# The last of eight gates moved out of the attention loop, into the loop's drain, the feed-forward layer's tail and the convolutions

## The chip, the cores and the metric

The kernel runs on one NeuronCore of one Trainium2 chip. Its engines work side by side and wait for each other on semaphores: TensorE (PE, with its weight loads as PEld), VectorE (DVE), ScalarE (ACT), GpSimd (POOL) and SyncE (SP, which issues DMAs). The metric is the device time of one execution in microseconds (us), the median of several runs.

## The reference

Two transformer layers over x of 4 x 256 tokens by 256 channels. The input of every sublayer goes through a gate, so there are four gates. Cut to what matters:

```
# a gate: r is x, k and v are the side input f, time_emb the condition
tf    = sigmoid(sum(time_emb));  decay = exp(-exp(w)) * (0.5 + 0.5*tf)
ek    = exp(min(k, 30));         ekv = ek * v
nf, df = forward  scans over tokens:  a = a*decay + ekv_t ;  b = b*decay + ek_t
nb, db = the same scans backward
euk   = exp(min(u + k, 30))
num   = nf + nb - ekv + euk*v ;  den = df + db - ek + euk
gate  = sigmoid(r) * num / max(den, 1e-8) * (0.8 + 0.2*tf)

layer 0:  x += attention(gate0(x))           16 heads of 16, causal softmax
          x += ternary_ffn(gate1(x))          256 -> 1024 -> 256, quantised
layer 1:  x += ssd(gate2(x))                  in-projection, convolution of width 4, chunked
                                              state space with 64 heads, gated norm, out-projection
          x += moe(gate3(x))                  8 experts, top 2
```

Only sigmoid(r) depends on x. The rest of a gate (scans, numerator, denominator, quotient) depends on inputs alone and can be computed at any time before it is used.

## The kernel before

Channels lie on the 128 partitions (2 tiles of 128), the 1024 tokens on the free axis in two halves of 512. A **gate** in what follows is one of eight pieces of work, i = 2m + c, for gate m = 0..3 of the reference and token half c = 0, 1. Its result, the quotient, goes to R[:, m, c]. Gate 7 (m = 3, c = 1) is therefore used last of all, in `gate_tiles` ahead of the experts.

On VectorE a gate is cut in steps (`gate_step(i, k)`), each on 128 x 1024 elements in float32. Step 1 is the forward and the backward scan of the denominator (L959 and L962, with a small product at L961 between them), step 2 the same two scans of the numerator, step 0 the denominator's sum (L966), step 3 two instructions for the numerator (L968, L969), step 5 two of a Newton step on the reciprocal (L973, L974), and step 6 the product into R (L976). ScalarE supplies what they read: `decay` (the decay matrix), `scaled_inputs`, `bonus` (the exponential with u), and `reciprocal_guess` (three activations over 128 x 1024, L549 to L551).

The order of instructions on each engine is written out by hand; there is no scheduler. The attention is a loop over 32 **units** u: unit u is 4 of the 16 heads (u mod 4) for one tile of 128 queries (u // 4). Tiles with odd number look at 256 keys and those with even number at 128. In iteration u

- PE does scores(u+1) (L1534, L1538), the transposition of unit u-1 (L1553), the values of unit u-2 (L1571, L1578), and after every fourth unit a projection of 16 matmuls (L1469);
- DVE does `inverse_sums` in odd u (L1037), `maxima(u)` (L1050), every fourth unit `add_attention` (L1033, which adds a projection to x and so waits for it), then the gate parts, and in even u `normalise` (L1042);
- ACT does the exponentials of unit u (`weigh`, L614), the copy of the transposed unit u-1 (L601), the turned sums (L605), and its own gate parts.

scores(u+1) waits until unit u-1's exponentials are done, because it overwrites their bank. Which gate parts go with which unit is set by PARTS: part n belongs to gate i = 1 + n // 5 with k = n % 5, and DVE does for k = 0, 1, 2, 3 the steps 0, 2, 3 and 5 with 6, and for k = 4 step 1 of the next gate. There are 35 parts for 32 units, so three units (TWICE = 6, 15, 24) have two.

After unit 31 comes the **drain** (the last transposition, values, projection and additions), then the feed-forward layer over 8 token tiles in a software pipeline of 14 stages s, then the state space sublayer: dt (L1196 to L1200), six convolutions (L1208; XBC_ORDER), during which ACT applies silu to each convolved tile (L753) and to the gate bank of one token tile (`gate_silu`, L742), whose bank PE (`gate_in`, L1755) can then refill; then the chunk loop (`front`, from L1234), and last the experts, whose weights are fetched while they compute. The scratch area `arena` (30 K words a partition) is shared by hand between the stages: in the kernel before, the feed-forward layer's buffers lie over the gates' inputs fT, fc, ek, ekv and their sums, so a gate can't be under way while that layer runs.

## Time and profile before

| | us |
|---|---|
| median of 3 runs | 668.86 (668.79 to 670.04) |
| time of the profiled execution | 668.92 |
| its span (first to last instruction) | 667.1 |
| PE busy | 530.3 (79%) |
| DVE busy | 410.8 (62%) |
| ACT busy | 371.0 (56%) |
| POOL busy | 147.9 (22%) |

1.8 us lie between the profiled execution's span and its time. In the span the attention takes from about 42 to 224 us, the feed-forward layer until about 304, the in-projection and convolutions until 345, the chunk loop until 465, and the rest is routing and experts. Times in the rows below are counted from the start of the span. Busy shares of the whole span mix these stages, so they say little of one; what a stage is worth is read in its own stretch.

### The profile page before, as it was taken

How to read it: one execution, taken by the hardware profiler on the slowest of the kernel's cores; microseconds unless marked ns; L12 is line 12 of the kernel's file. 1: busy time of each engine (PE TensorE's matmuls, PEld its weight loads, DVE VectorE, ACT ScalarE, POOL GpSimd, SP SyncE). 2: the span in 40 equal slices, each digit the busy share in tenths (PEclk: the TensorE clock that was granted, in tenths of full speed). 3: DMA queues.
4: the chain of work that ended last, by engine and by line, in shares of the span. 5: the costliest groups of instructions: out<-in, count | busy, mean ns of one | idle time of the engine just before them, and what ended most of it. 6: DMA issues, size and time to landing. Idle time of an engine off the chain costs nothing.

```text
span 667.1 us, 14042 instructions
## 1 busy us (share of the span) xinstructions
PE 530.3 (79%) x5730; PEld 384.8 (58%) x5732; DVE 410.8 (62%) x620; ACT 371.0 (56%) x793; POOL 147.9 (22%) x115
## 2 busy tenths in 40 slices
PE   0386988887687766579989999998469999999980
PEld 0153655665465652364664566557469999996560
DVE  7989999999988477975955646546811111111223
ACT  7996888978876407656667565585312222222212
POOL 1000000000000127830229666220022222222110
PEclk9985599787867898989999999999679999999995
DMA  8600000000000000000000000000579999888815
GB/s 330 215 2 0 1 1 1 2 1 1 1 1 33 1 0 1 0 1 1 2 2 3 2 3 2 3 2 2 190 274 420 420 420 352 321 311 322 345 78 197
DMA packets 18335, 71.18 MB, mean 107 GB/s; under 512 B 4832, under 2 KB 9696, under 8 KB 14688
## 3 DMA queue, kind: packets, MB, share of 16 engines
q1 hardware_dynamic: 15120, 64.00, 25.1%
q0 software_dynamic: 1920, 5.25, 2.1%
q10 hardware_dynamic: 1232, 1.06, 0.5%
q8 instruction: 45, 0.74, 0.5%
q14 instruction: 18, 0.15, 0.1%
HBM read 65.57 MB, written 4.72 MB: 105 GB/s over the span
## 4 chain that ended last, share of the span: by engine, by line
PE 52%; DVE 35%; ACT 6%; issue 4%; DMA 2%; POOL 1%; SPq 0%; DVEq 0%; POOLq 0%; ACTq 0%
PE PS L1469 37%; DVE arena L962 5%; DVE arena L959 4%; DVE nmx L1050 3%; PE PS L1982 2%; PE PS L1799 2%; PE PS L2051 2%; PE PS L1755 1%; PE PS L1617 1%; DVE R L976 1%; DVE arena L974 1%; DVE arena L973 1%; DVE arena L968 1%; DVE arena L969 1%; ACT arena L781 1%
## 5 line engine op out<-in xcount | busy, mean ns | idle before, releaser
L1469 PE MATMUL PS<-arena 128*128 128x128 f32 (+5 forms) x1374 | 160.1, 293 | 17.7 <-DVE arena L1147 10.1
L1469 PEld LDWEIGHTS PS<-arena 128*128 128x128 f32 (+4 forms) x1376 | 126.7, 164 | 44.6 <-issue 25.9
L614 ACT ACTIVATE arena<-PS,nmx 128x128 f32<-128x128 f32 (+1 forms) x128 | 52.1, 423 | 30.2 <-DVE nmx L1050 30.2
L1417 DVE TENSOR_TENSOR R<-arena,PS 128x128 f32<-128x128 f32 x16 | 4.6, 288 | 88.2 <-ACT arena L878 88.2
L389 POOL TENSOR_SCALAR arena<-ident,gcol 128x128 f32<-128x128 f32 x4 | 2.4, 602 | 213.5 <-DMA gcol<-in_gcol 213.5
L481 POOL DMA_INDIRECT ypair<-arena,oid x20 | 19.8, 988 | 121.9 <-ACT arena L884 121.9
L1534 PE MATMUL PS<-arena 32*128 32x128 f32 (+1 forms) x128 | 23.7, 454 | 27.0 <-ACT arena L614 27.0
L449 POOL TENSOR_TENSOR arena<-arena 128x1024 f32<-128x1024 f32 x16 | 37.8, 2371 | 32.8 <-DVE arena L1235 26.8
L1469 PE MATMUL PS<-arena,R 128*128 128x256 f32 x192 | 44.2, 380 | 0.6 <-ACT arena L884 0.6
L1469 PEld LDWEIGHTS PS<-arena,R 128*128 128x128 f32 x192 | 35.2, 190 | 5.1 <-issue 1.0
L962 DVE TENSOR_TENSOR_SCAN arena<-dmat,arena 128x1023 f32<-128x1023 f32 x16 | 37.6, 2348 | 0.6
L1553 PE MATMUL PS<-ident,arena 128*128 128x128 f32 x192 | 35.5, 336 | 0.5 <-ACT arena L601 0.5
L884 ACT ACTIVATE arena<-PS 128x256 f32<-128x256 f32 x20 | 7.7, 384 | 49.4 <-PE PS L1469 36.1
L1534 PEld LDWEIGHTS PS<-arena 32*128 32x128 f32 x128 | 11.6, 220 | 35.9 <-ACT arena L614 33.2
L1050 DVE TENSOR_REDUCE nmx<-PS 128x4 f32<-128x512 f32 (+1 forms) x32 | 30.6, 958 | 1.6 <-PE PS L1538 0.5
L1553 PEld LDWEIGHTS PS<-ident,arena 128*128 128x128 f32 x192 | 29.6, 177 | 3.2 <-issue 2.2
L471 POOL DMA_INDIRECT arena<-arow,gid x20 | 19.6, 981 | 49.5 <-DVE gid L1390 43.7
L871 ACT ACTIVATE arena<-PS 128x512 f32<-128x512 f32 (+1 forms) x20 | 11.9, 597 | 32.7 <-PE PS L1469 26.8
L860 ACT ACTIVATE arena<-PS 128x256 f32<-128x256 f32 x20 | 7.7, 384 | 37.8 <-PE PS L1963 37.8
L614 ACT ACTIVATION_READ_ACCUMULATOR arena<-PS,nmx 128x1 f32 x128 | 26.6, 208 | 0.0
L670 ACT ACTIVATE arena<-PS,oscale 128x512 f32<-128x512 f32 x16 | 10.6, 682 | 24.6 <-PE PS L1469 24.1
L1208 DVE SCALAR_TENSOR_TENSOR arena<-PS,convw,arena 128x1020 f32<-128x1020 f32 (+2 forms) x18 | 23.0, 1276 | 0.7
(312 smaller groups left out, 1181.0 us busy)
## 6 DMA issues: line engine op xcount, KB each, us to landing
arena<-in_moe SPq DMA_DIRECT2D x23, 1408.0 KB, 7.2
arena<-in_moe SPq DMA_DIRECT2D x23, 768.0 KB, 9.6
inproj<-in_inproj SPq DMA_DIRECT2D x1, 1344.0 KB, 10.5
arena<-in_fT SPq DMA_DIRECT2D x2, 512.0 KB, 4.2
R<-in_w1T SPq DMA_DIRECT2D x1, 1024.0 KB, 7.7
R<-in_w2T SPq DMA_DIRECT2D x1, 1024.0 KB, 9.7
R<-in_w3T SPq DMA_DIRECT2D x1, 1024.0 KB, 11.7
xT<-in_xT SPq DMA_DIRECT2D x1, 1024.0 KB, 13.7
```

The costliest lines, as they stand in the source:

```text
L449: pool.tensor_tensor(part, part, gm[i % 2].unsqueeze(1).broadcast_to([P, 32, Q]), ALU.mult).then_inc(S["pool_m"], 1)
L471: pool.indirect_dma_start(xin[:, s % XR, :], None, arow, bass.IndirectOffsetOnAxis(ap=gid[:, b:b + 1], axis=0)).then_inc(ld_xin[s % XR], 16)
L481: pool.indirect_dma_start(ypair, bass.IndirectOffsetOnAxis(ap=oid[:, b:b + 1], axis=0), yb[s % YB], None).then_inc(st_y, 16)
L614: sc.activation(pr[u % 2][:, j, 0:n], PS[:, 2 * (u % 2) + j // 2, (j % 2) * 256:(j % 2) * 256 + n], ACT.Exp, bias=nmx[:, u % 2, j:j + 1], ...
L959: done(v.tensor_tensor_scan(y, dmat[:, 0:N], x, 0.0, ALU.mult, ALU.add))
L962: done(v.tensor_tensor_scan(y[:, 0:N - 1][:, ::-1], dmat[:, 1:N][:, ::-1], y[:, 0:N - 1][:, ::-1], y[:, N - 1:N], ALU.mult, ALU.add), "dve ...
L1050: done(v.tensor_reduce(nmx[:, u % 2, :], src[:, :, 0:P * (tt + 1)], X, ALU.max, negate=True), "dve_max")
L1208: done(v.scalar_tensor_tensor(o[:, :, back:], s[:, :, 0:T - back], convw[:, k, 3 - back:4 - back], o[:, :, back:], ALU.mult, ALU.add), "dv ...
L1469: last = mm(dst, l, r, start=(n == 0), stop=(n == len(pairs) - 1))
L1534: mm(PS[:, 2 * (u % 2) + j // 2, (j % 2) * 256:(j % 2) * 256 + n], qT[j % 2][r:r + 32, ch, ct, t:t + P], kT[r:r + 32, ch, ct, (b % 2) * T: ...
L1553: last = nc.tensor.transpose(PSB[:, 4 * HALF + c:4 * HALF + c + P], pr[u % 2][:, j, k * P:(k + 1) * P], ident[:])
L1799: last = mm(PS[cols[c], r, :], ugt[rows, rows], stp[i % 2][rows, 32 * c + 16 * j:32 * c + 16 * j + 16, :].rearrange("p h t -> p (h t)"), s ...
```

## The change

Gate 7 leaves the loop. PARTS now holds 30 parts, one for each of the units 0 to 29; units 30 and 31 have none, and unit 29's part has only ScalarE's work. Step 1 of gate 7 is split: the forward scan goes between unit 31's maxima and the last `inverse_sums`, the backward scan after `add_attention(6)`; step 0 follows the last `normalise`. Step 2 is split as well: the forward scan at stage 12 of the feed-forward layer, ahead of the last addition (L1139), the backward one behind `gate(2, 1)`. Step 3 lies between the two halves of the dt computation, and steps 5 and 6 behind the last convolution. On ACT `reciprocal_guess(7)` goes ahead of dt's softplus, and the four scalings of `outproj` that stood there move behind the loop over the convolved tiles, ahead of the last three `gate_silu`. POOL's four products for `diag` (L453) now wait for the last backward scan, and its first `steps` for gate 7's step 3. The arena is laid out anew so that the feed-forward layer's buffers miss gate 7's inputs. The load of gb and gcol, for which POOL's products for `diagg` (L389) wait, now waits for gate 6's numerator instead of gate 7's quotient.

```
-        fT, fc, ek, ekv = halves(0), halves(2), halves(4), halves(6)
+        fT = [arena[:, o * K:(o + 1) * K] for o in (7, 4)]
+        fc = [arena[:, o * K:(o + 1) * K] for o in (8, 5)]
+        ek, ekv = halves(9), halves(11)
-        sums = [arena[:, w:w + K] for w in range(8 * K, 12 * K, K)]
-        ekq, ekvq = arena[:, 12 * K:13 * K], sb("ekvq", [P, N])
+        sums = [arena[:, w:w + K] for w in range(0, 4 * K, K)]
+        ekq, ekvq = arena[:, 6 * K:7 * K], sb("ekvq", [P, N])
-        FO = K + 2 * CT * P
+        FO = 8 * K + 2 * CT * P
...
-            sp.wait_ge(S["dve_R"], 8)
-            sp.wait_ge(S["act_euk"], 16)
+            sp.wait_ge(S["dve_num"], 7)
+            sp.wait_ge(S["act_euk"], 14)
             load(gb, a["gb"], "gb")
             load(gcol[:], a["gcol"], "gb")
...
             pool.wait_ge(ld["ssd"], 12 * 16)
+            pool.wait_ge(S["dve_scan"], 16)
             for k in range(XT):
                 last = pool.tensor_scalar(diag[:, k, :], ident[:], dskip[:, k:k + 1], None, ALU.mult)
             last.then_inc(S["pool_made"], 1)
             pool.wait_ge(S["dve_dt"], 2)
+            pool.wait_ge(S["dve_num"], 8)
             steps(0)
...
             done(sc.activation(anegb[:], alog[:], ACT.Exp), "act_exw")
-            for k in range(XT):
-                sc.activation(outproj[:, k, :], outproj[:, k, :], ACT.Copy, scale=normw[:, k:k + 1]).then_inc(S["act_opw"], 1)
+            reciprocal_guess(7)
             act.wait_ge(S["dve_dtx"], 1)
...
                 if n:
                     gate_silu(n - 1)
+            for k in range(XT):
+                sc.activation(outproj[:, k, :], outproj[:, k, :], ACT.Copy, scale=normw[:, k:k + 1]).then_inc(S["act_opw"], 1)
             for i in range(5, NT):
                 gate_silu(i)
...
+            act.wait_ge(S["dve_R"], 8)
             for q in range(4):
                 decays(0, q)
...
-                if k == 4 and i < 7:
+                if k == 4 and i < 6:
                     gate_step(i + 1, 1)
...
+            scan_forward(7, 1)
             inverse_sums(15)
             normalise(14)
             add_attention(6)
+            scan_back(7, 1)
             normalise(15)
+            gate_step(7, 0)
             add_attention(7)
...
+                if s == NT + 4:
+                    scan_forward(7, 2)
             gate(2, 1)
+            scan_back(7, 2)
...
+            gate_step(7, 3)
             dve.wait_ge(S["act_sp2"], 1)
...
+            gate_step(7, 5)
+            gate_step(7, 6)
...
-TWICE = (6, 15, 24)
-PARTS = [range(u + sum(k < u for k in TWICE), u + 1 + sum(k <= u for k in TWICE)) for u in range(32)]
+PARTS = [range(u, min(u + 1, 6 * FRAME)) for u in range(32)]
```

(scan_forward and scan_back are the two halves of what gate_step did in steps 1 and 2.) The line numbers of the changed kernel differ; in the rows that follow, L963, L965 and L970 are the forward scan, the small product and the backward scan (they are listed as SCALAR_TENSOR_TENSOR), L982 is step 0, L984 and L985 step 3, L989, L990 and L992 steps 5 and 6, L1066 maxima, L1053 `inverse_sums`, L1058 `normalise` and L1049 `add_attention`.

VectorE, from unit 28's maxima to the last addition of the attention's drain, before. Here L1050 is maxima, L1033 add_attention, L1042 normalise, L1037 inverse_sums.

```order
L1050 TENSOR_REDUCE nmx<-PS 128x4
L1033 TENSOR_TENSOR xT<-xT,PS 128x2x128
L959 SCALAR_TENSOR_TENSOR arena<-dmat,ekvq 128x1024
L961 TENSOR_TENSOR arena<-arena,rdq 128x4
L962 SCALAR_TENSOR_TENSOR arena<-dmat,arena 128x1023
...
L1050 TENSOR_REDUCE nmx<-PS 128x4
L968 SCALAR_TENSOR_TENSOR arena<-arena 128x1024
L969 TENSOR_TENSOR arena<-arena 128x1024
L1050 TENSOR_REDUCE nmx<-PS 128x4
L973 SCALAR_TENSOR_TENSOR arena<-arena 128x1024
L974 SCALAR_TENSOR_TENSOR arena<-arena 128x1024
L976 SCALAR_TENSOR_TENSOR R<-arena 128x1024
```

The same place after the change, from behind unit 28's maxima on; the gate steps of unit 28 are now gate 6's.

```order
L1049 TENSOR_TENSOR xT<-xT,PS 128x2x128
L989 SCALAR_TENSOR_TENSOR arena<-arena 128x1024
L990 SCALAR_TENSOR_TENSOR arena<-arena 128x1024
L992 SCALAR_TENSOR_TENSOR R<-arena 128x1024
L1058 TENSOR_TENSOR arena<-PS,rT 128x256
L1053 RECIPROCAL rinv<-esum 128x8
L1066 TENSOR_REDUCE nmx<-PS 128x4 x2
L1058 TENSOR_TENSOR arena<-PS,rT 128x256
L1053 RECIPROCAL rinv<-esum 128x8
L1066 TENSOR_REDUCE nmx<-PS 128x4
L963 SCALAR_TENSOR_TENSOR arena<-dmat,arena 128x1024
L965 TENSOR_TENSOR arena<-arena,rdq 128x4
```

Units 29 to 31 had steps 2, 3 and 5 with 6 between (and around) their maxima; now the maxima of units 29 and 30 follow each other, and gate 7's first scan comes only after unit 31's.

VectorE from the last `gate` product of the feed-forward layer to the first convolution, after the change (L997 is the product of `gate(2, 1)`, L1214 and L1215 prepare constants, L1218, L1222 and L1223 are dt, L1231 is a convolution); before, the row of L970 and those of L984 and L985 were not there and all others stood in this order.

```order
L997 TENSOR_TENSOR A<-A,R 128x2x512
L970 SCALAR_TENSOR_TENSOR arena<-dmat,arena 128x1023
L1214 TENSOR_SCALAR anegb<-anegb 128x64
L1215 MEMSET eps 128x1
L1218 TENSOR_TENSOR arena<-PS,dtb 128x512
L984 SCALAR_TENSOR_TENSOR arena<-arena 128x1024
L985 TENSOR_TENSOR arena<-arena 128x1024
L1222 SCALAR_TENSOR_TENSOR arena<-arena 128x512
L1223 TENSOR_TENSOR arena<-arena,anegb 128x512
L1231 SCALAR_TENSOR_TENSOR arena<-PS,convw,arena 128x4x255
```

Three instructions thus stand ahead of the convolutions that did not. ScalarE at the last convolved tiles, after the change (L752 is silu of a convolved tile, L741 `gate_silu`, L756 the scalings of outproj); before, the four last `gate_silu` stood together as one row `x4` and the scalings far ahead of them.

```order
L752 ACTIVATE arena<-arena 128x1024
L741 ACTIVATE R<-PS 128x512
L752 ACTIVATE arena<-arena 128x1024
L741 ACTIVATE R<-PS 128x512
L756 ACTIVATE outproj<-outproj,normw 128x256 x4
L741 ACTIVATE R<-PS 128x512 x3
```

The scalings now separate `gate_silu(4)` from `gate_silu(5)`.

## Rows read from the trace of the kernel before

**Rows 1.** Two stretches: length, busy PE, PEld, DVE, ACT, POOL, clock, DMA share, GB/s

```profile
60.00:213.00 153.00, 119.99 (x1091) 84.19 (x1090) 145.99 (x143) 122.43 (x352) 0.00 (x0) 0.78 0.00 1
190.00:195.00 5.00, 4.99 (x41) 3.27 (x38) 4.83 (x6) 2.25 (x11) 0.00 (x0) 0.50 0.01 3
```

**Rows 2.** Waits from 60 to 213 us: total, times, longest

```profile
ACT arena L614 <- DVE nmx L1050: 26.5, 17, 4.1
```

**Rows 3.** Timeline of DVE, 186 to 213 us: start, duration, instruction [idle before]

```profile
186.89 2.29 DVE L959 TENSOR_TENSOR_SCAN arena<-dmat,arena 128x1024 f32<-128x1024 f32 x1
...
189.42 2.35 DVE L962 TENSOR_TENSOR_SCAN arena<-dmat,arena 128x1023 f32<-128x1023 f32 x1
...
193.22 1.22 DVE L966 SCALAR_TENSOR_TENSOR arena<-arena 128x1024 f32<-128x1024 f32 x1
...
196.96 0.42 DVE L1033 TENSOR_TENSOR xT<-xT,PS 128x256 f32<-128x256 f32 x1 [1.25 <-PE PS L1469]
...
203.02 1.22 DVE L1050 TENSOR_REDUCE nmx<-PS 128x4 f32<-128x1024 f32 x1
...
208.05 1.23 DVE L973 SCALAR_TENSOR_TENSOR arena<-arena 128x1024 f32<-128x1024 f32 x1
...
212.53 1.22 DVE L1050 TENSOR_REDUCE nmx<-PS 128x4 f32<-128x1024 f32 x1
```

**Rows 4.** Timeline of DVE: two earlier additions of a projection

```profile
87.33 0.42 DVE L1033 TENSOR_TENSOR xT<-xT,PS 128x256 f32<-128x256 f32 x1
...
107.72 0.42 DVE L1033 TENSOR_TENSOR xT<-xT,PS 128x256 f32<-128x256 f32 x1 [0.81 <-PE PS L1469]
```

**Rows 5.** Timeline of PE: two projections, unit 31's scores, its transposition

```profile
83.44 2.10 PE L1469 MATMUL PS<-arena 128*128 128x128 f32 x16
...
193.53 3.32 PE L1469 MATMUL PS<-arena 128*128 128x128 f32 x16
...
206.26 1.07 PE L1534 MATMUL PS<-arena 32*128 32x256 f32 x4 [2.58 <-ACT arena L614]
...
216.78 1.07 PE L1553 MATMUL PS<-ident,arena 128*128 128x128 f32 x8 [0.29 <-ACT arena L601]
```

**Rows 6.** Timeline of DVE in the drain

```profile
215.82 0.20 DVE L1037 RECIPROCAL rinv<-esum 128x8 f32<-128x8 f32 x1 [2.07 <-ACT arena L614]
...
220.93 0.42 DVE L1042 TENSOR_TENSOR arena<-PS,rT 128x256 f32<-128x256 f32 x1 [3.04 <-ACT rT L605]
...
223.57 0.42 DVE L1033 TENSOR_TENSOR xT<-xT,PS 128x256 f32<-128x256 f32 x1 [2.21 <-PE PS L1469]
```

**Rows 7.** Timeline of DVE, feed-forward layer's end to the chunk loop

```profile
302.96 0.42 DVE L1139 TENSOR_TENSOR xT<-xT,PS 128x256 f32<-128x256 f32 x1 [4.01 <-PE PS L1673]
...
308.13 0.69 DVE L1196 TENSOR_TENSOR arena<-PS,dtb 128x512 f32<-128x512 f32 x1 [1.57 <-PE PS L1469]
...
310.91 0.69 DVE L1199 SCALAR_TENSOR_TENSOR arena<-arena 128x512 f32<-128x512 f32 x1 [2.09 <-ACT arena L718]
...
346.59 0.29 DVE L1234 COPY arena<-PS 128x128 f32<-128x128 f32 x1 [6.39 <-PE PS L1469]
```

**Rows 8.** Timeline of ACT: of a guess, the scalings, the last convolved tile

```profile
179.19 1.15 ACT L550 ACTIVATE arena<-arena,tiny 128x1024 f32<-128x1024 f32 x1
...
306.01 1.69 ACT L711 ACTIVATE outproj<-outproj,normw 128x256 f32<-128x256 f32 x4
...
340.23 1.06 ACT L753 ACTIVATE arena<-arena 128x1024 f32<-128x1024 f32 x1 [1.03 <-DVE arena L1208]
```

**Rows 9.** Timelines of POOL and DVE where both read the scratch memory

```profile
362.14 3.63 POOL L441 TENSOR_TENSOR inproj<-arena,step 128x2048 f32<-128x2048 f32 x1
...
362.36 3.82 DVE L1260 TENSOR_TENSOR arena<-arena,R 128x384 f32<-128x384 f32 x1
...
289.80 3.30 POOL L453 TENSOR_SCALAR ekvq<-ident,dskip 128x128 f32<-128x128 f32 x4
...
290.02 0.69 DVE L1165 TENSOR_SCALAR arena<-arena 128x1024 bf16<-128x1024 f32 x1 [0.56 <-ACT arena L680]
```

More of the change, by code:

```diff
@@ L161, in build @@
         rT = sb("rT", [P, 2, 256])
-        gb = arena[:, 0:H]
-        diagg = arena[:, K:K + 2 * CT * P].rearrange("p (a l n) -> p a l n", a=CT, l=2)
-        FO = K + 2 * CT * P
+        gb = arena[:, 7 * K:8 * K]
+        diagg = arena[:, 8 * K:8 * K + 2 * CT * P].rearrange("p (a l n) -> p a l n", a=CT, l=2)
+        FO = 8 * K + 2 * CT * P
         def ffn(k, words=K):
@@ L322, in _ @@
             load(condT[:], a["condT"], "cond")
-            load(fT[:, 0, :], a["fT"][:, 0, :], "f")
-            load(fT[:, 1, :], a["fT"][:, 1, :], "f1")
+            load(fT[0], a["fT"][:, 0, :], "f")
+            load(fT[1], a["fT"][:, 1, :], "f1")
             for w, n in enumerate(("w1T", "w2T", "w3T")):
@@ L530, in by_condition @@
             def by_condition(c):
-                f4, s4 = (w[:, c, :].rearrange("p (a b t) -> p a b t", a=CT, b=B // NCH) for w in (fc, fT))
+                f4, s4 = (w[c].rearrange("p (a b t) -> p a b t", a=CT, b=B // NCH) for w in (fc, fT))
                 for b in range(B // NCH):
@@ L541, in bonus @@
                     cols = slice(ct * HALF, (ct + 1) * HALF)
-                    sc.activation(sums[0][:, cols], fT[:, c, cols], ACT.Exp, bias=wu[:, m, 1, ct:ct + 1])\
+                    sc.activation(sums[0][:, cols], fT[c][:, cols], ACT.Exp, bias=wu[:, m, 1, ct:ct + 1])\
                         .then_inc(S["act_euk"], 1)
@@ L917, in smallest @@
                 dve.wait_ge(ld[("f", "f1")[c]], 16)
-                done(v.tensor_scalar(ek[:, c, :], fT[:, c, :], 30.0, None, ALU.min), "dve_fmin")
+                done(v.tensor_scalar(ek[:, c, :], fT[c], 30.0, None, ALU.min), "dve_fmin")
             dve.wait_ge(S["act_cond"], 1)
@@ L936, in values_in @@
                 dve.wait_ge(S["act_ek"], 2 * c + 2)
-                done(v.tensor_tensor(ekv[:, c, :], ek[:, c, :], fc[:, c, :], ALU.mult), "dve_fc")
+                done(v.tensor_tensor(ekv[:, c, :], ek[:, c, :], fc[c], ALU.mult), "dve_fc")
             def first_input():
@@ L945, in first_input, with scan_sides, scan_forward, scan_back @@
                                      dq[:, 0, :, 0:B // NCH].unsqueeze(3).broadcast_to(by_batch), ALU.mult))
+            def scan_sides(i, k):
+                m, c = divmod(i, 2)
+                nf, df = sums[1:3]
+                return m, c, dmats[i % 2], *((ekq, df, "act_ekq") if k == 1 else (ekvq[:], nf, "act_ekvq"))
+            def scan_forward(i, k):
+                m, c, dmat, x, y, name = scan_sides(i, k)
+                dve.wait_ge(S["act_decay"], 4 * (i + 1))
+                if k == 2:
+                    dve.wait_ge(S[name], 4 * (i + 1))
+                elif i:
+                    dve.wait_ge(S[name], 4 * i)
+                done(v.tensor_tensor_scan(y, dmat[:, 0:N], x, 0.0, ALU.mult, ALU.add))
+                ends = y.rearrange("p (a b t) -> p a b t", a=CT, b=2)[:, :, :, T - 1]
+                done(v.tensor_tensor(ends, ends, rdq[:, m, :, 2 * c:2 * c + 2], ALU.mult))
+            def scan_back(i, k):
+                m, c, dmat, x, y, name = scan_sides(i, k)
+                done(v.tensor_tensor_scan(y[:, 0:N - 1][:, ::-1], dmat[:, 1:N][:, ::-1], y[:, 0:N - 1][:, ::-1], y[:, N - 1:N],
+                                          ALU.mult, ALU.add), "dve_scan")
             def gate_step(i, k):
@@ L950, in gate_step @@
                 g, nf, df, db = sums
-                x, y, name = (ekq, df, "act_ekq") if k == 1 else (ekvq[:], nf, "act_ekvq")
-                dmat = dmats[i % 2]
                 if k in (1, 2):
-                    dve.wait_ge(S["act_decay"], 4 * (i + 1))
-                    if k == 2:
-                        dve.wait_ge(S[name], 4 * (i + 1))
-                    elif i:
-                        dve.wait_ge(S[name], 4 * i)
-                    done(v.tensor_tensor_scan(y, dmat[:, 0:N], x, 0.0, ALU.mult, ALU.add))
-                    ends = y.rearrange("p (a b t) -> p a b t", a=CT, b=2)[:, :, :, T - 1]
-                    done(v.tensor_tensor(ends, ends, rdq[:, m, :, 2 * c:2 * c + 2], ALU.mult))
-                    done(v.tensor_tensor_scan(y[:, 0:N - 1][:, ::-1], dmat[:, 1:N][:, ::-1], y[:, 0:N - 1][:, ::-1], y[:, N - 1:N],
-                                              ALU.mult, ALU.add), "dve_scan")
+                    scan_forward(i, k)
+                    scan_back(i, k)
                 if k == 0:
@@ L967, in gate_step @@
                 if k == 3:
-                    done(v.scalar_tensor_tensor(g, g, E30, fc[:, c, :], ALU.min, ALU.mult))
+                    done(v.scalar_tensor_tensor(g, g, E30, fc[c], ALU.min, ALU.mult))
                     done(v.tensor_tensor(nf, nf, g, ALU.add), "dve_num")
```

## The prediction

> **What bounds the kernel now.** I read the busy time by stretches first. Between 60 and 213 us, which is nearly all of the attention loop, VectorE is busy 145.99 of 153 us, and its 143 groups are each followed by some 0.03 us in which the next instruction is started, so it hardly ever stands still. PE is busy 119.99 us at a mean granted clock of 0.78, ScalarE 122.43 us [rows 1]. The waits say the same from the other side: ScalarE's exponentials wait 26.5 us in 17 places for VectorE's maxima [rows 2]. In this loop VectorE sets the pace, and work taken off it there should shorten it. VectorE's own timeline then shows where that stops: at 196.96 it waits 1.25 us for a projection, and after unit 31's maxima at 212.53 it has no more than short instructions between waits of 2.07, 3.04 and 2.21 us [rows 3, 6]. The drain is the chain of PE and ScalarE, and VectorE has room in it. It has room again at 302.96 (4.01 us), at 308.13 (1.57), at 310.91 (2.09) and at 346.59 (6.39) [rows 7].
>
> **What leaves the loop.** A pair of scans takes 4.91 us of VectorE: the forward one starts at 186.89, the backward one at 189.42 and lasts 2.35, and 0.03 follow [rows 3]. An instruction over 128 x 1024 takes 1.22 and a gap, 1.26 [rows 3]. A whole gate is two pairs and six such instructions, 17.4 us. How much of it the loop gets back depends on where the loop stops being VectorE's. That place is unit 29's maxima at 203.02: the scores of unit 31 start on PE at 206.26, 2.58 us after PE went idle, as soon as the exponentials that follow those maxima are done, and from there PE runs through to the drain [rows 3, 5]. Steps 3, 5 and 6, which VectorE did behind 203.02 (the last from 208.05), delay unit 31's maxima to 212.53, but PE then waits only 0.29 us for it, at 216.78 [rows 3, 5]. So these 6.3 us are nearly worthless in that place.
>
> Ahead of 203.02 stood three parts that are no longer there: step 1 (4.91), step 0 (1.26) and step 2 (4.91), together **11.1 us**.
>
> **What comes in the way of the 11.1.** One part for each unit means that at most places VectorE is ahead of its old time, by the part or parts it has not done yet. Where it must wait for a projection, the lead can be lost.
> - The first addition, 87.33, has a lead of the three instructions of steps 5 and 6, 3.8 us, so VectorE arrives at 83.5. The projection runs from 83.44 to 85.54 and its inputs don't come sooner [rows 4, 5]: 2.0 us are lost.
> - The second, 107.72, waited 0.81; behind the loss above VectorE no longer arrives early there: 0.8 come back [rows 4].
> - At the third, in unit 16, two parts are outstanding (step 2 with 4.9, step 3 with 2.5), and with the 1.2 lost so far the lead is 6.2 us. Whether it then waits depends on the level of PE's clock: the same 16 matmuls take 2.10 us at the high level and 3.32 at the low one [rows 5], and in the stretch of the longer one the granted clock is 0.50, that is 1.2 GHz [rows 1]. I make it 0 to 1.2, and take 0.6.
> - At the sixth, 196.96, VectorE waited 1.25 [rows 3]. Unit 26's exponentials follow ScalarE's own gate part, and by my walk from them PE ends the projection 1.3 us ahead of VectorE at the high level, 2.1 behind it at the low one. That gives back about 1.1 or costs about 1.0: I take 0.
>
> 11.1 - 2.0 + 0.8 - 0.6 = **9.3 us** less up to unit 29's maxima, between 8.2 and 10.4.
>
> **The drain.** The 0.29 us at 216.78 go [rows 5], since unit 31's maxima come early; behind that, ScalarE's table load is no longer in front of the last copy. I take **0.5 us**. What is added there: the forward scan (2.53 with the small product) against the wait of 2.07. The sums it makes 0.5 late are needed only after unit 31's values, so that costs nothing. The backward scan (2.38) lies in the 3.04, step 0 (1.26) in the 2.21 [rows 6]. If that cover were gone, these 6.2 us would come on the path one for one.
>
> **Feed-forward layer to chunk loop.** The forward scan of step 2 (2.5) lies in the 4.01 us at 302.96 [rows 7] and costs nothing. The backward scan (2.38) stands behind `gate(2, 1)` against 1.57 us and a short wait for ScalarE ahead of it: dt starts about 0.5 late. Step 3 is 2.52 us against a wait of 2.09 [rows 7]: together the convolutions start 0.5 + 2.5 - 2.1 = 0.9 late. ScalarE's guess (three activations such as the 1.15 one) takes 3.4 us where the scalings took 1.69 [rows 8]; it ends at 309.4, just as dt ends, and its softplus is 0.6 late, less than VectorE. VectorE runs from one convolution to the next, so the delay stays, 0.8 at the last one, where ScalarE waits for it (1.03 us at 340.23 [rows 8]). Behind ScalarE's wait stands `gate_silu(4)`, which frees the bank for PE's seventh gate tile, and now the scalings (1.69) stand ahead of `gate_silu(5)`, for which PE's eighth waits: another 0.3. Steps 5 and 6 (3.8) lie in the 6.39 us at 346.59 [rows 7] at no cost. Sum: **1.1 us** later. POOL's `diag` now comes at 308 instead of 289.80; the chunk loop needs it only behind 350.
>
> 668.9 (the profiled execution's own time, 0.06 over the median) - 9.3 - 0.5 + 1.1 = **660.2 us**.
>
> **A rule that speaks against it.** At 362.36 a product of VectorE over 384 columns with two inputs in the scratch memory takes 3.82 us, longer than the 1.22 of one over 1024, and ends just after POOL's instruction that began at 362.14 and lasted 3.63 [rows 3, 9]. On the other hand VectorE's L1165 at 290.02 took its 0.69 in the midst of POOL's four short products [rows 9]. The change puts VectorE's steps with two such inputs beside POOL's short products twice: the four for `diagg` come some 4 us after gate 6's numerator, which is unit 28 with steps 5 and 6, and the four for `diag` come with step 3. The price is between 0 (the row at 290.02) and 0.8 us for each of POOL's eight (3.30 / 4). I take 0 in the sum, since the nearest row is of the same short products. The Trainium skill (SBUF — State Buffer, Who interferes with whom) makes the pair of ports that VectorE and GpSimd share an exclusive lock, held for a whole instruction, also against VectorE's instructions with two inputs from SBUF. By that rule the sum would be about 663. The row at 362.36 agrees, the one at 290.02 does not.
>
> **Rivals.**
> - *The lock*: three of VectorE's instructions at unit 28 and two to four at step 3 each wait for one product. For seven at 0.8 that would be 5.6; as POOL is held up as well, about half: 660.2 + 2.9 = 663.1. Chance 0.15.
> - *All of the lead*: PE and ScalarE come forward as VectorE does, no new wait, both old ones (0.81, 1.25) go: 668.9 - 13.2 - 0.7 + 1.1 = 656.1. For it speaks PE's idle time (119.99 of 153); against it, the first projection's fixed time. Chance 0.12.
> - *Low clock in the last units*: projections of 3.32 at units 16 and 28 and waits of PE's own at the scores cost the lead another 2 to 3: 662.5 to 663.5. Chance 0.11.
> - *Slower*: PE at the low level throughout the loop. The clock of 0.78 is a low share of 0.44; with the factor 3.32 / 2.10 = 1.58, 119.99 us are 95.6 at the high level and 151 at the low one; with half of PE's 33 us of waits that is 167.5 for 153, and the time 684. It decides once the low share is over 0.74. Against it: a shorter loop has PE's same work closer together. Chance 0.03.
> - *No change*: the loop is bound by ScalarE's and PE's chain and VectorE only fills it. 145.99 of 153 speaks against it. 668 to 670. Chance 0.03.
>
> The forecast has 0.56 and its own range is 658.5 to 662. The range of 8 in 10 is **656.5 to 664.0**. A measurement of this kernel tells 0.2% (1.3 us) from no change; faster than that 0.94, within 0.03, slower 0.03.
>
> **What would show it.** Right: maxima of unit 29 at 192.5 to 195, of units 29 to 31 with no scan between them; the loop's VectorE waits longer than before at the first and third additions; the last addition of the drain at about 214; the wait before `front(0)` near 3.7 us instead of 6.39; stages from the chunk loop on unchanged in length. Wrong: VectorE's gate instructions of more than 1.3 us at unit 28 or at step 3 (the lock); a clock well under 0.78 in the loop; a chunk loop whose length moves by over 1 us because POOL and VectorE meet otherwise in it, which no term here holds.

## The result, and the profile after

The changed kernel takes **660.86 us** (median of 8 runs, 660.02 to 665.4), the kernel before 668.68 in the same comparison (8 runs, 666.55 to 670.04). The ratio is 0.9893, with a 95% interval of 0.9874 to 0.9913: faster by 1.1%, some 7.8 us. The forecast was 660.2 with a range of 656.5 to 664.0. The profiled execution took 660.65; its span is 658.8 instead of 667.1. The total fits, but two of its parts don't, and they cancel.

Of the page of the changed kernel, the busy time and the granted clock in 40 slices:

```profile
span 658.8 us, 14046 instructions
...
PE 523.9 (80%) x5730; PEld 378.8 (57%) x5732; DVE 408.6 (62%) x620; ACT 369.8 (56%) x793; POOL 150.2 (23%) x115
...
PEclk9995799897888989799978999999579999999995
```

Its stretch in the attention loop that answers to [rows 1] (length, busy PE, PEld, DVE, ACT, POOL, clock, DMA share, GB/s):

```profile
60.00:202.00 142.00, 111.61 (x1112) 78.73 (x1112) 133.34 (x134) 121.10 (x360) 3.61 (x4) 0.85 0.02 5
```

VectorE is still what is busy all the time (133.34 of 142 us), but TensorE's clock is 0.85 where it was 0.78. VectorE's timeline, for [rows 3, 4, 6, 7] (start, duration, instruction [idle before]):

```profile
83.68 0.69 DVE L1066 TENSOR_REDUCE nmx<-PS 128x4 f32<-128x512 f32 x1
84.40 0.42 DVE L1049 TENSOR_TENSOR xT<-xT,PS 128x256 f32<-128x256 f32 x1
...
186.13 0.42 DVE L1049 TENSOR_TENSOR xT<-xT,PS 128x256 f32<-128x256 f32 x1 [0.43 <-PE PS L1495]
...
191.11 2.48 DVE L1066 TENSOR_REDUCE nmx<-PS 128x4 f32<-128x1024 f32 x2
...
210.91 0.42 DVE L1049 TENSOR_TENSOR xT<-xT,PS 128x256 f32<-128x256 f32 x1 [0.95 <-PE PS L1495]
...
288.62 0.42 DVE L1158 TENSOR_TENSOR xT<-xT,PS 128x256 f32<-128x256 f32 x1 [1.49 <-PE PS L1699]
...
294.29 0.69 DVE L1218 TENSOR_TENSOR arena<-PS,dtb 128x512 f32<-128x512 f32 x1
295.02 1.23 DVE L984 SCALAR_TENSOR_TENSOR arena<-arena 128x1024 f32<-128x1024 f32 x1
296.28 1.27 DVE L985 TENSOR_TENSOR arena<-arena 128x1024 f32<-128x1024 f32 x1
...
333.55 0.29 DVE L1260 COPY arena<-PS 128x128 f32<-128x128 f32 x1 [2.94 <-PE PS L1495]
...
343.36 0.29 DVE L1260 COPY arena<-PS 128x128 f32<-128x128 f32 x1 [5.68 <-PE PS L1495]
...
354.17 0.56 DVE L1281 TENSOR_TENSOR arena<-PS,arena 128x384 f32<-128x384 f32 x1 [7.42 <-PE PS L1495]
...
355.68 1.05 DVE L1286 TENSOR_TENSOR arena<-arena,R 128x384 f32<-128x384 f32 x1
```

The reader is to walk down the two timelines side by side. Unit 29's maxima stood at 203.02 [rows 3] and stand at 191.11: 11.9 us. The drain's last addition stood at 223.57 [rows 6] and stands at 210.91: 0.75 more. The last addition of the feed-forward layer stood at 302.96 and stands at 288.62: another 1.7. `front(0)` stood at 346.59 [rows 7] and stands at 333.55, so 1.3 are given back. Then comes what no term held: `gated(0)` stood at 360.86 and stands at 354.17, so 6.35 us are lost in the first tile of the chunk loop. VectorE waits 5.68 and 7.42 us there, where it had waited 3.25 and 3.49. The product that follows took 3.82 [rows 9] and takes 1.05, and 1.6 come back by `gated(1)`. Sum: 11.9 + 0.75 + 1.7 - 1.3 - 6.35 + 1.6 = 8.3, the difference of the spans.

The first tile by stretches, columns as in [rows 1]; the kernel before, whose `front(0)` is at 346.59:

```profile
344.00:350.00 6.00, 4.53 (x86) 2.39 (x77) 3.22 (x6) 3.53 (x6) 4.36 (x2) 1.00 0.00 0
350.00:356.00 6.00, 5.24 (x31) 1.94 (x35) 2.59 (x6) 5.52 (x11) 6.00 (x3) 1.00 0.01 3
356.00:362.00 6.00, 6.00 (x200) 3.41 (x200) 2.44 (x4) 4.78 (x9) 6.00 (x3) 1.00 0.01 3
```

and the changed one, with `front(0)` at 333.55:

```profile
330.00:336.00 6.00, 4.52 (x105) 2.96 (x101) 2.93 (x6) 4.05 (x7) 3.40 (x1) 1.00 0.01 1
336.00:342.00 6.00, 5.12 (x20) 1.16 (x13) 1.60 (x3) 4.28 (x8) 6.00 (x4) 0.65 0.01 3
342.00:348.00 6.00, 6.00 (x21) 2.03 (x23) 3.22 (x6) 2.01 (x4) 4.77 (x2) 0.50 0.00 0
348.00:354.00 6.00, 6.00 (x195) 3.23 (x187) 0.00 (x0) 3.93 (x7) 3.66 (x2) 0.71 0.00 0
```

The granted clock was 1.00 (2.4 GHz) throughout and now falls to 0.50 (1.2 GHz) for nearly 14 us (the lost shares of the last three stretches, 0.35, 0.50 and 0.29 of 6 us each, are half of 13.7). What TensorE did before, in the changed kernel:

```profile
323.78 3.70 PE L1781 MATMUL PS<-inproj,A 128*32 128x128 f32 x128 [0.99 <-ACT R L741]
328.46 4.03 PE L1781 MATMUL PS<-inproj,A 128*32 128x128 f32 x128 [0.98 <-ACT R L741]
...
335.76 1.09 PE L1825 MATMUL PS<-arena,ugt 64*64 64x512 f32 x8 [1.36 <-ACT arena L766]
337.73 2.02 PE L1495 MATMUL PS<-arena 32*128 32x512 f32 x2 [0.88 <-DVE arena L1267]
```

and before the change, where only the second wait is another (0.30 instead of 0.98):

```profile
337.83 3.70 PE L1755 MATMUL PS<-inproj,A 128*32 128x128 f32 x128 [0.99 <-ACT R L742]
341.83 3.70 PE L1755 MATMUL PS<-inproj,A 128*32 128x128 f32 x128 [0.30 <-ACT R L742]
...
348.74 1.09 PE L1799 MATMUL PS<-arena,ugt 64*64 64x512 f32 x8 [1.30 <-ACT arena L765]
350.76 1.12 PE L1469 MATMUL PS<-arena 32*128 32x512 f32 x2 [0.94 <-DVE arena L1241]
```

### The profile page after: what moved, and what is told of

It reads as the page before. It is cut to its first block, busy times and chain, and to the rows that moved or that the text cites. A ratio compares the mean times of both kernels' runs of the same rounds, so it can differ in the third digit from the quotient of the medians.

```text
span 658.8 us, 14046 instructions
## 1 busy us (share of the span) xinstructions
PE 523.9 (80%) x5730; PEld 378.8 (57%) x5732; DVE 408.6 (62%) x620; ACT 369.8 (56%) x793; POOL 150.2 (23%) x115
## 3 DMA queue, kind: packets, MB, share of 16 engines
HBM read 65.57 MB, written 4.72 MB: 107 GB/s over the span
## 4 chain that ended last, share of the span: by engine, by line
PE 46%; DVE 39%; ACT 8%; issue 4%; DMA 2%; POOL 1%; DVEq 0%; POOLq 0%; ACTq 0%
PE PS L1495 32%; DVE arena L970 5%; DVE arena L963 4%; DVE nmx L1066 4%; DVE arena L1231 4%; PE PS L1825 2%; PE PS L2008 2%; PE PS L2077 2%; ACT arena L782 1%; DVE R L992 1%; DVE arena L985 1%; DVE arena L990 1%; DVE arena L984 1%; DVE arena L989 1%; DVE arena L982 1%
## 5 line engine op out<-in xcount | busy, mean ns | idle before, releaser
L1495 PEld LDWEIGHTS PS<-arena 128*128 128x128 f32 (+4 forms) x1376 | 125.1, 163 | 46.2 <-issue 28.5
L485 POOL DMA_INDIRECT ypair<-arena,oid x20 | 19.8, 990 | 121.3 <-ACT arena L886 121.3
L970 DVE TENSOR_TENSOR_SCAN arena<-dmat,arena 128x1023 f32<-128x1023 f32 x16 | 37.6, 2348 | 0.6
L1579 PE MATMUL PS<-ident,arena 128*128 128x128 f32 x192 | 33.4, 322 | 0.3 <-ACT arena L605 0.3
L1066 DVE TENSOR_REDUCE nmx<-PS 128x4 f32<-128x512 f32 (+1 forms) x32 | 30.6, 958 | 2.3 <-PE PS L1564 1.3
L873 ACT ACTIVATE arena<-PS 128x512 f32<-128x512 f32 (+1 forms) x20 | 11.9, 597 | 32.3 <-PE PS L1495 26.4
L1579 PEld LDWEIGHTS PS<-ident,arena 128*128 128x128 f32 x192 | 27.6, 169 | 3.2 <-issue 2.5
L774 ACT ACTIVATE arena<-PS 128x512 f32<-128x512 f32 x28 | 16.7, 597 | 16.3 <-PE PS L1495 16.3
L1281 DVE TENSOR_TENSOR arena<-PS,arena 128x384 f32<-128x384 f32 x8 | 4.5, 558 | 33.7 <-PE PS L1495 33.7
```

What stands on the lines that cost most here:

```text
L485: pool.indirect_dma_start(ypair, bass.IndirectOffsetOnAxis(ap=oid[:, b:b + 1], axis=0), yb[s % YB], None).then_inc(st_y, 16)
L774: sc.activation(sst[:, c - 1, :], bank(4 + (c - 1) % 2), ACT.Copy).then_inc(S["act_s"], 1)
L970: done(v.tensor_tensor_scan(y[:, 0:N - 1][:, ::-1], dmat[:, 1:N][:, ::-1], y[:, 0:N - 1][:, ::-1], y[:, N - 1:N], ALU.mult, ALU.add), "dve ...
L1066: done(v.tensor_reduce(nmx[:, u % 2, :], src[:, :, 0:P * (tt + 1)], X, ALU.max, negate=True), "dve_max")
L1495: last = mm(dst, l, r, start=(n == 0), stop=(n == len(pairs) - 1))
L1579: last = nc.tensor.transpose(PSB[:, 4 * HALF + c:4 * HALF + c + P], pr[u % 2][:, j, k * P:(k + 1) * P], ident[:])
```

## The experiments

Medians of single runs hide which stage moved. So each profile is also read by two lengths: from unit 0's maxima to unit 29's (the loop; 160.9 us before), and from the first convolution to `gated(1)` (60.6 before, 65.6 after). Twelve kernels ran:

| kernel | median us | ratio to before, 95% | loop | convolutions to gated(1) |
|---|---|---|---|---|
| a_again | 662.37 | 0.9896 (0.9865 to 0.9926) | 148.1 | 65.6 |
| e_scal | 660.20 | 0.9866 (0.9835 to 0.9897) | 152.9 | 63.6 |
| e_inloop | 668.96 | 1.0001 (0.9978 to 1.0025) | 161.8 | 60.6 |
| e_drop | 657.11 | 0.9821 (0.9790 to 0.9853) | 148.1 | 60.8 |
| e_fill | 658.75 | 0.9856 (0.9833 to 0.9878) | 148.1 | 61.7 |
| e_both | 658.84 | 0.9852 (0.9827 to 0.9876) | 150.2 | 61.7 |
| e_two | 666.22 | 0.9968 (0.9949 to 0.9987) | 155.5 | 60.8 |
| e_diag | 662.11 | 0.9910 (0.9884 to 0.9936) | 148.0 | 65.5 |
| c_fill | 671.53 | 1.0037 (1.0024 to 1.0050) | 161.8 | 62.5 |
| e_gate | 660.26 | 0.9868 (0.9844 to 0.9892) | 153.0 | 61.7 |
| e_seg | 658.97 | 0.9858 (0.9832 to 0.9885) | 148.0 | 60.9 |
| e_best | 669.56 | 1.0008 (0.9986 to 1.0030) | 153.0 | 71.1 |

**The changed kernel again.**

> The changed kernel once more, so that what one profile shows can be told from what is there each time. In the first profile the loop ended 12.75 us sooner than before (a sum of 9.3 was forecast), and the chunk loop lost 4.7 us in its first tile, where the granted clock fell to 0.50 for about 338 to 351 us. Theory A (both belong to the kernel): again 660 to 661.5, with the low clock in the first tile of the chunk loop and the gap of about 5.7 us ahead of front(1). Theory B (the clock falls by chance from one execution to the next): another profile has the low stretch elsewhere or not at all, front(1) some 7.4 us behind front(0) as before, and the total moves by up to 4 us with it.

Every landmark came within 0.03 us of the first profile, the low clock included. But the six runs lie between 660.13 and 663.94. Theory A holds for the profile. The median is 0.9 above its range, and that another execution can run otherwise was shown by the next kernel.

**The scalings elsewhere.**

```
             for n in range(6):
+                if n == 3:
+                    for k in range(XT):
+                        sc.activation(outproj[:, k, :], outproj[:, k, :], ACT.Copy, scale=normw[:, k:k + 1]).then_inc(S["act_opw"], 1)
                 if n + 2 < 6:
                     conv_start(n + 2)
```

> The changed kernel with ScalarE's four scalings of the output projection (1.70 us) taken from between gate_silu(4) and gate_silu(5) and put ahead of the sixth conv_start, where ScalarE waits 2.73 us. Theory A, they cause the loss in the chunk loop: they make PE idle for 0.98 instead of 0.30 us before its eighth gate tile, and this is what lets the granted clock fall soon after. Then the clock stays at 1.00 through the first tile, front(0) comes 0.5 to 0.7 sooner, and the total falls by 3 to 5, to about 656.5. Theory B, they cost only what PE waits: 0.5 to 0.7 sooner, the low stretch stays, 660.2. Theory C, nothing, since the wait was hidden: 660.9.

`front(0)` came 34.13 us behind the first convolution instead of 34.46: 0.33, the forecast's 0.3 for the scalings. TensorE's second wait stayed at 0.98, and there was a low stretch again (clocks of 0.85, 0.50 and 0.80 in three neighbouring stretches of 6 us, some 10 us in all), so the scalings are not its cause: A is out. The total can't be told from that of the changed kernel. The profile shows something else. Up to the convolutions the code is that of the changed kernel, yet its loop ran like this:

```profile
82.41 0.69 DVE L1067 TENSOR_REDUCE nmx<-PS 128x4 f32<-128x512 f32 x1
85.08 0.42 DVE L1050 TENSOR_TENSOR xT<-xT,PS 128x256 f32<-128x256 f32 x1 [1.99 <-PE PS L1496]
...
189.61 0.42 DVE L1050 TENSOR_TENSOR xT<-xT,PS 128x256 f32<-128x256 f32 x1 [1.25 <-PE PS L1496]
...
194.63 2.48 DVE L1067 TENSOR_REDUCE nmx<-PS 128x4 f32<-128x1024 f32 x2
```

Here is the wait at the first addition that the forecast had put at 2.0. The reason is the clock in the stretch just before, e_scal:

```profile
72.00:84.00 12.00, 11.51 (x93) 8.88 (x94) 10.79 (x10) 11.94 (x30) 0.00 (x0) 0.55 0.00 1
```

the changed kernel, and behind it the kernel before:

```profile
72.00:84.00 12.00, 9.54 (x108) 7.24 (x100) 11.66 (x11) 11.94 (x33) 0.00 (x0) 0.86 0.00 1
72.00:84.00 12.00, 11.09 (x88) 8.37 (x89) 11.65 (x11) 11.94 (x30) 0.00 (x0) 0.52 0.01 1
```

**Gate back in the loop, new layout kept.**

```
-PARTS = [range(u, min(u + 1, 6 * FRAME)) for u in range(32)]
+TWICE = (6, 15, 24)
+PARTS = [range(u + sum(k < u for k in TWICE), u + 1 + sum(k <= u for k in TWICE)) for u in range(32)]
```

and the moved steps and the scalings at their old places.

> The last gate is back in the attention loop and the scalings are back at their old place; what stays of the change is the other layout of the arena and the load of gb one gate sooner. Theory A, layout and load are worth nothing: 668.7, as before the change, within 0.3%. Theory B, they are part of the gain (the loop's gain was 12.75 where 9.3 were forecast; the gb product on POOL ran 2.4 us elsewhere): 665 to 667.

The ratio is 1.0001: layout and load are worth nothing. Theory A. Its profile has a short low stretch at the first tile of the chunk loop (clocks of 0.87 and 0.84 in two neighbouring stretches of 6 us, some 3.5 us in all), with the second of TensorE's waits at 0.30: without the moved steps the clock can fall there too.

**The moved steps left out.**

> Work is left out: of the last gate only ScalarE's shares in the loop and the final product (1.23 us) remain; both pairs of scans, the denominator, the numerator, the guess and the correction are gone. It prices the steps that the change moved. By the forecast they cost 0 in the drain and 0.8 between feed-forward layer and chunk loop (0.5 from the backward scan, 2.5 against a wait of 2.1 for step 3), so this is 0.8 to 1.1 below the changed kernel, about 660. Rival: the moved steps also cost where no term stood (a lower clock behind them, POOL's products beside them): 2 to 5 below, 656 to 659. Nothing at all: the same 660.9.

Its loop is the changed kernel's, so the two profiles can be set against each other. The first convolution starts at 297.99 instead of 299.09 and `front(0)` comes at 332.48 instead of 333.55: 1.1 us, where the forecast had 0.8 for these steps (its 1.1 holds 0.3 for the scalings, which stay moved here). But the total is 3.8 to 5.3 us below, and the rest of that lies behind `front(0)`, where the low stretch is short:

```profile
336.00:342.00 6.00, 5.34 (x25) 2.02 (x25) 1.15 (x4) 4.84 (x9) 6.00 (x3) 0.72 0.01 3
342.00:348.00 6.00, 6.00 (x197) 3.37 (x196) 2.68 (x4) 4.78 (x9) 6.00 (x3) 1.00 0.01 3
```

The rival holds: the moved steps cost where the forecast had no term. TensorE's second wait is 0.30 again, though the scalings stand where the changed kernel has them:

```profile
323.39 3.70 PE L1772 MATMUL PS<-inproj,A 128*32 128x128 f32 x128 [0.98 <-ACT R L740]
327.40 4.03 PE L1772 MATMUL PS<-inproj,A 128*32 128x128 f32 x128 [0.30 <-ACT R L740]
```

So it is the moved steps that widen it. They put the last convolution 0.7 us later against TensorE: ScalarE waits 1.71 us for it in the changed kernel, and 1.03 in e_drop and before the change.

**Matmuls to nowhere in TensorE's waits.**

```
+            def keep_busy(n):
+                for _ in range(n):
+                    mm(bank(4), ident[:], A[:, 0, 0:HALF], start=True, stop=True)
...
             for i in range(4, NT):
+                if i >= 6:
+                    pe.wait_ge(S["dve_cv"], 5)
+                    keep_busy(1)
                 gate_in(i)
...
             segments(0, 0)
+            keep_busy(2)
             segments(0, 1)
+            keep_busy(1)
```

> The changed kernel with five more matmuls over 512 columns (0.45 us each at the high level), written to a free bank and never read, in four waits of TensorE: one each ahead of the seventh and eighth gate tile (waits of 0.99 and 0.98), two ahead of the second half of segments(0) (1.36) and one ahead of state(0, 1) (0.88). Theory A, the granted clock falls in the first tile of the chunk loop because TensorE stands still so often just ahead of it: the clock stays at 1.00 there, front(1) comes 7.4 to 8 behind front(0) instead of 9.8 and gated(0) 13 to 14 instead of 20.6, and the total falls by 3 to 5, to 656 to 658. Theory B, the clock falls whatever these waits are (the phase of the clock decides): no gain, the low stretch is still there, 660 to 661.5.

One of the places is not the one that the expectation names. TensorE, from the fifth gate tile on:

```profile
323.92 3.70 PE L1785 MATMUL PS<-inproj,A 128*32 128x128 f32 x128 [0.99 <-ACT R L741]
327.55 1.13 PE L1773 MATMUL PS<-A,ident 128*128 128x512 f32 x2
328.61 1.95 PE L1785 MATMUL PS<-inproj,A 128*32 128x128 f32 x64
```

A tile is 64 matmuls. The wait of 0.99 is ahead of the fifth and stays; the first added matmul fills the 0.98, ahead of the seventh, and the second stands ahead of the eighth, where there was little to fill (the last two tiles took 4.03 us together, 3.70 before the change). In the profile of e_fill the low stretch is gone:

```profile
336.00:342.00 6.00, 6.00 (x29) 1.79 (x27) 2.58 (x4) 4.21 (x9) 6.00 (x4) 1.00 0.01 4
342.00:348.00 6.00, 6.00 (x130) 2.77 (x130) 3.22 (x6) 5.04 (x10) 6.00 (x3) 1.00 0.00 0
```

`front(1)` is 7.98 behind `front(0)`, `gated(0)` 14.9 behind it (20.6 without), though `front(0)` itself is 1.0 late by the added matmuls and the product at the end of `gated(0)` takes 3.28 again. The span is 654.7. The stretch went as theory A said, but the median is above its 656 to 658: it is 2.1 below the changed kernel's first and 3.6 below its second, where 3 to 5 were expected.

e_both adds the scalings ahead of the sixth `conv_start`:

> The matmuls of e_fill and the scalings ahead of the sixth conv_start (that alone was 660.20, with the low stretch still there, while its front(0) came 0.32 sooner behind the last silu of the convolutions). Theory A: as e_fill and 0.3 less, about 656.5. Theory B: 660.

No low stretch, and no further gain: `front(0)` comes 35.3 us behind the first convolution with the scalings moved and without, where 0.3 less and 656.5 in all had been expected. The 17 runs of the four kernels with these matmuls (e_fill, e_both and the two that follow) have a median of 659.5, the 14 of the changed kernel 661.4. That is 1.9 us less, with a 95% interval of 0.7 to 3.6 by resampling.

**Which of the waits.** The first two matmuls alone, and the other three alone:

> The changed kernel with only the matmuls ahead of the seventh and eighth gate tile (waits of 0.99 and 0.98); those at segments(0) and state(0, 1) are out. e_fill, with all five, was 658.75 and its profile had no low stretch; each matmul of 512 columns took 1.06 us there, not the 0.45 forecast, since each is two records. Theory A, the wait that the change widened (0.30 to 0.98 ahead of the eighth tile) is what lets the clock fall: no low stretch here, 658.5 to 659.5. Theory B, the two waits behind (1.36 and 0.88) are: the low stretch stays, 661 to 662.5.

> The counterpart: only the matmuls at segments(0) (1.36) and state(0, 1) (0.88). Theory A (the gate waits decide): the low stretch stays, 661 to 662.5. Theory B (the waits just ahead of the first tile decide): no low stretch, 658 to 659.5. If both this and e_gate are without it, it is the sum of the waits that counts and either half is enough.

Neither profile has the low stretch, so either half of the matmuls was enough in them. With one profile each, and low stretches of 3 to 14 us in those without matmuls, this does not show that either half is always enough. e_gate's median is above its range; its profile ran through the longer loop (153.0), which may be why, and its length from the convolutions to `gated(1)` is that of e_fill. As control, the same matmuls in the kernel before:

> A control: the kernel before the change with the matmuls of e_fill at the same places. Its own first profile had the high level from 310 us through the whole chunk loop, with waits of 0.99, 0.30, 1.30 and 0.94 us at these places. Theory A, the low stretch behind these places is a cost that the change brought (its second wait is 0.98): here nothing is to be won, and the matmuls delay TensorE by up to 1.5 us: 668.7 to 670. Theory B, the kernel before had the low stretch too in a part of its executions (the profile of e_inloop has about 6 us of it there), so the matmuls win here as well: 666 to 668.

Slower by 0.37% (0.24 to 0.50). The matmuls put `front(0)` 1.9 us later behind the first convolution (36.1 for 34.2); in e_fill it was 0.9 (35.3 for 34.5), and there the total fell all the same. What wins about 2 us behind the change costs 2.8 before it, so most of the loss in the chunk loop belongs to the change. This is theory A of the control; its price, 671.5 for 668.7 to 670, was above the range.

**Two steps back in the loop.**

```
-PARTS = [range(u, min(u + 1, 6 * FRAME)) for u in range(32)]
+PARTS = [range(u + (u > 6), min(u + 1 + (u >= 6), 6 * FRAME + 1)) for u in range(32)]
```

with steps 1 and 0 of the last gate taken out of the drain.

> The changed kernel with steps 1 and 0 of the last gate back in the attention loop (4.91 and 1.26 us), and with them the first of the three doubled places, unit 6; steps 2, 3, 5 and 6 stay moved. Theory A, parts ahead of the last maxima are worth their own time save what a wait for a projection takes: with the doubling at unit 6 VectorE has no lead at the first addition and loses nothing there, so 6.2 less 1.0 to 2.0 more than the changed kernel, 665.5 to 667. Theory B, in the drain these two steps cost as much as in the loop: the same as the changed kernel, 661. Theory C, they are worth more than their time in the loop by the clock of TensorE: over 668.

666.22 is inside theory A. Its profile, though with the changed kernel's code from behind the drain on and TensorE's second wait at 0.99, had a short low stretch only (clocks of 0.91 and 0.81 in two neighbouring stretches of 6 us), and convolutions to `gated(1)` took 60.8. The low stretch is thus not equally long in each execution of that code.

**POOL's short products, four times over.**

```
+            for _ in range(3):
+                for k in range(XT):
+                    done(pool.tensor_scalar(diag[:, k, :], ident[:], dskip[:, k:k + 1], None, ALU.mult))
             for k in range(XT):
                 last = pool.tensor_scalar(diag[:, k, :], ident[:], dskip[:, k:k + 1], None, ALU.mult)
```

> The changed kernel with POOL's four products for diag (128 x 128, 3.95 us with VectorE beside them) made four times over, twelve more short products that lie beside step 3, the sums for the chunk loop and the first convolution. Theory A, POOL's products lock VectorE out of the scratch memory: each costs VectorE up to 0.8 us, half of it as POOL is held up too, so 5 to 10 us more, 666 to 671. Theory B, VectorE is hardly held (0.04 us per instruction as in the first profile) and POOL itself is stretched: 660.5 to 661.5.

POOL:

```profile
293.65 9.68 POOL L457 TENSOR_SCALAR ekvq<-ident,dskip 128x128 f32<-128x128 f32 x12 [18.60 <-DVE arena L973]
303.42 2.34 POOL L459 TENSOR_SCALAR ekvq<-ident,dskip 128x128 f32<-128x128 f32 x4
```

and VectorE beside it:

```profile
294.60 1.22 DVE L987 SCALAR_TENSOR_TENSOR arena<-arena 128x1024 f32<-128x1024 f32 x1
295.85 1.28 DVE L988 TENSOR_TENSOR arena<-arena 128x1024 f32<-128x1024 f32 x1
297.16 0.74 DVE L1225 SCALAR_TENSOR_TENSOR arena<-arena 128x512 f32<-128x512 f32 x1
...
298.72 7.83 DVE L1234 SCALAR_TENSOR_TENSOR arena<-PS,convw,arena 128x1020 f32<-128x1020 f32 x6
```

None of VectorE's is longer by more than 0.06 us. Theory B; the median, 662.11, is 0.6 above its range and can't be told from the changed kernel's.

**All together, and step 3 behind the convolutions.** Its matmuls have 256, 512 and 384 columns; `gate_step(7, 3)` stands ahead of `gate_step(7, 5)`.

> What the runs so far point to, together: matmuls sized to their waits (256 columns ahead of the last two gate tiles, 512 and 384 further on) instead of five of 1.06 us, which put front(0) 1.0 us later; the scalings ahead of the sixth conv_start (0.3); and step 3 of the last gate behind the convolutions with steps 5 and 6, so that these start 0.5 instead of 1.1 late. Sum: e_fill's 658.75 less 0.6 to 1.0, 0.3 and 0.6: 656.9 to 657.3. If step 3 behind the convolutions makes POOL's first step product late for the chunk loop (it waits for the numerator), 1 to 2 of it are lost: 658 to 659.

The ratio is 1.0008: all of the change's gain is gone, far outside what was expected. POOL, whose first step product waits for the numerator, is late:

```profile
334.03 4.24 POOL L443 TENSOR_TENSOR arena<-arena,step 128x2048 f32<-128x2048 f32 x1 [32.86 <-DVE arena L986]
338.23 4.61 POOL L443 TENSOR_TENSOR inproj<-arena,step 128x2048 f32<-128x2048 f32 x1
```

and it falls beside VectorE's steps 5 and 6:

```profile
334.80 4.55 DVE L991 SCALAR_TENSOR_TENSOR arena<-arena 128x1024 f32<-128x1024 f32 x1
339.38 4.54 DVE L993 SCALAR_TENSOR_TENSOR R<-arena 128x1024 f32<-128x1024 f32 x1
343.95 0.29 DVE L1261 COPY arena<-PS 128x128 f32<-128x128 f32 x1
```

Two instructions of 1.23 us take 4.55 and 4.54, each ending 1.1 us behind the end of one of POOL's. ScalarE's decays wait for `R`, TensorE stands 4.72 us for them, and the clock is 0.54, 0.50 and 0.54 in the three stretches of 6 us from 342 to 360. Against e_gate's profile, which has the same loop, the convolutions to `gated(1)` take 9.4 us more. The expectation priced POOL's lateness and not whom it would then meet.

## Why the prediction was right, and where only by luck

**That VectorE bounds the loop: right.** Layout alone gives nothing (e_inloop), the parts taken out give the gain, and two of them put back cost most of their time: 6.2 us of steps, 3.9 to 5.4 in the medians (e_two). That step 1 of a gate and the others cost nothing in the drain and in the feed-forward layer is shown by e_drop, whose drain (19.8 us) and feed-forward layer (77.7) are as long without them.

**The 9.3 us up to unit 29's maxima: mis-sized.** The pair of profiles gives 11.9 by position and 12.75 by the loop's length (160.86 to 148.10). The step that failed is "The projection runs from 83.44 to 85.54 and its inputs don't come sooner". They did: they are TensorE's own matmuls of iterations 6 and 7, and these ran at the low level in [rows 5]'s execution (clock 0.52 from 72 to 84 us) and mostly at the high one in the other (0.86). The same code gave both cases. Of the ten profiles with this loop, six took 148.0 to 148.1 and show no wait at the first addition, one took 150.2, and three took 152.9 to 153.0, with 1.99 to 2.05 of wait there, 1.32 or 1.33 at the fifth addition and 1.25 to 1.27 at the sixth. Against the mean of the three with the gate in the loop (161.5), that is a gain of 8.6 in the forecast's own case, 13.4 in the commoner one and 11.8 on average. The forecast was made from one execution of before and took its clock as a property of the kernel. Its own signs say the same: maxima of unit 29 at 192.5 to 195, a wait at the first addition and the drain's last addition at about 214 are e_scal's profile (194.63, 1.99, 213.78) and not the first one (191.11, none, 210.91), and neither waits at the third addition (0.6 in the sum). What the forecast gave a chance of 0.12, the whole lead kept with 13.2 in the loop, is what the commoner case did there (13.4).

**The sixth addition at 0:** 0.8 of its 1.25 came back in the first profile, and in e_scal 1.25 stayed. The doubt between +1.1 and -1.0 was right and so was its cause.

**The drain:** 0.75 for a forecast of 0.5, and the moved steps fit into its waits. **The feed-forward layer** gained 1.7 that no term held. With the longer loop the same stage gained 0.2 (e_scal), so this too goes with how the clock fell and not with the moved scan.

**Feed-forward layer to chunk loop, 1.1:** right. It was 1.3 in the pair; its parts are 1.1 for the steps (e_drop; 0.8 forecast) and 0.33 for the scalings (e_scal; 0.3 forecast).

**The chunk loop "unchanged in length": wrong.** This was put at nothing without a reason. It lost 4.75 us net in the pair (6.35, less 1.6). The text had named this among its wrong signs, with another cause (POOL and VectorE). The cause shown is TensorE's clock: TensorE is busy all of 342 to 354 at 0.50 and 0.71. What makes it fall is shown in part. The moved steps delay `gate_silu(4)` and so widen the wait ahead of the seventh gate tile from 0.30 to 0.98. In the three profiles with 0.30 there and no added matmuls the low time was 0, 3.5 and 3.4 us (before, e_inloop, e_drop), in the five with 0.98 or 0.99 it was 13.7, 13.7, 13.7, 10.2 and 3.4 (the changed kernel twice, e_diag, e_scal, e_two). In the four with matmuls in the waits (e_fill, e_both, e_gate, e_seg) it was 0, and before the change there is nothing to win by them (c_fill). So the wide wait goes with a long low stretch, but not each time; why e_two's is short stays open.

**The lock: rightly left out of the sum, though by a weak row.** The zero rested on L1165 at 290.02, which has one input in the scratch memory; e_diag shows it for instructions with two. VectorE lost 0.04 to 0.06 per instruction, with four products or sixteen (e_diag). It was POOL that waited: its four products took 3.61 at `diagg` and 3.95 at `diag`, against 2.34 beside the first convolutions, and 7.30 in e_inloop. POOL's long products do hold VectorE: 3.82 [rows 9], and 4.55 and 4.54 in e_best. The Trainium skill (SBUF — State Buffer, Who interferes with whom) says that whoever issues first holds the pair for its whole instruction. The long products agree; behind short ones VectorE, which goes from one instruction to the next, hardly ever waits in these traces.

So 660.2 is right by compensation. In the profiled execution, 2.6 us more up to unit 29's maxima than forecast, 2.0 more in drain and feed-forward layer, 0.2 less up to the chunk loop and 4.75 lost in it make 660.2 into 660.5, for the 660.65 that it took. The changed kernel's second comparison, 662.37, lies in the range as well.

Two numbers of the rivals are wrong in themselves and touch nothing above. In "slower", 0.44 is a share of the time and was used as one of the work: 119.99 us are 100.6 at the high level and 159 at the low one, the time would be 691, and the case decides from a low share of 0.72. In "all of the lead" the drain has 0.7 without a reason where the forecast has 0.5.

## What to carry to other kernels

Take the clock in a profile as that of one execution: where a term hangs on TensorE's level, price it at both levels and look at more than one profile of the same code before calling a time fixed. When steps are moved into an engine's waits, follow what their delay does to TensorE's own short waits: here one of four grew from 0.30 to 0.98 us, and 4.75 us were lost behind them in the profile. A few matmuls to nowhere in those waits won about 2 us back, and cost 2.8 where the wait had not grown; so try them against a control. Before moving a step behind which another engine waits, ask whom that engine's work will then meet: 2.5 us of step 3, put some 32 us later, cost more than the whole change had won.
